# State-space phase with scans and step-times-B of 1024 columns, and ScalarE's silu and softplus behind all decays of a unit

## The reference

```python
uc = depthwise_conv4(x @ Win_u.T) + convb;  u = silu(uc);  z = x @ Win_z.T
dtr, Bm, Cm = split(u @ Wx.T, [8, 16, 16])
dt = softplus(dtr @ Wdt.T + bdt);  A = -exp(Alog)          # A is 256 x 16
h  = exp(dt_t * A) * h + (dt_t * u_t) * B_t                # 512 steps, for each channel and state
y_t = sum_n h[:, n] * C_t[n]
y  = (y + u * D) * silu(z);  out = y @ Wout.T
```

## Time and profile before

| | us |
|---|---|
| median of three runs | 2219.79 |
| the profiled execution | 2225.48 |
| its span, first to last instruction | 2223.7 |
| start, up to VectorE's first dt | 42.3 |
| unit (0,0), first part | 42.3 to 97.5 |
| the loop's rhythm (14 units) | 97.5 to 970.9 |
| rest of the last unit | 970.9 to 1031.6 |
| end of the last batch | 1031.6 to 1056 |
| attention and experts | 1056 to 2223.7 |

### The profile page before, as it was taken

The page is one execution under the profiler, slowest core; times in us unless marked ns, Lnnn a source line. Parts: engine busy times, 40 slices in busy tenths (PEclk is TensorE's granted clock), DMA queues, the critical chain, the costliest instruction groups (busy, mean ns, idle before and its releaser), DMA issues.

```text
span 2223.7 us, 29267 instructions
## 1 busy us (share of the span) xinstructions
PE 1614.2 (73%) x7664; PEld 938.7 (42%) x7664; DVE 1626.8 (73%) x2538; ACT 1174.6 (53%) x1906; POOL 1233.7 (55%) x1097
## 2 busy tenths in 40 slices
PE   3677676766677666765376887877879888897888
PEld 1445454544455444544133343443434434343443
DVE  3999999999999999996262738456384654837455
ACT  4565555656565555561146391754727357282751
POOL 2777677777777677774336280643717346181541
PEclk8888777877888777775567598898989989899999
DMA  4212022121212011120301000000100001000000
GB/s 149 82 77 84 21 82 81 76 95 76 95 76 91 21 74 81 76 91 12 115 6 36 11 27 11 16 35 16 36 8 9 34 16 36 16 10 26 11 0 15
DMA packets 39620, 107.23 MB, mean 48 GB/s; under 512 B 4128, under 2 KB 30048, under 8 KB 34368
## 3 DMA queue, kind: packets, MB, share of 16 engines
q1 hardware_dynamic: 39520, 106.24, 12.6%
HBM read 92.99 MB, written 8.65 MB: 46 GB/s over the span
## 4 chain that ended last, share of the span: by engine, by line
issue 25%; POOL 13%; PE 6%; DVE 4%; DMA 2%; ACT 1%; SPq 0%; POOLq 0%; DVEq 0%; ACTq 0%
POOL pp L1892 9%; DMA k<-k_scratch 1%; DVE mx L1583 1%; PE pbk L1224 1%; PE po L1231 1%; PE pa L1218 1%; PE og L1167 1%; PE scores L1119 1%; PE scores L1117 1%; POOL ln_r L1822 0%; DVE rec L1611 0%; POOL kp L1855 0%; ACT pt L1414 0%; POOL rotk L1851 0%; PE scores L1147 0%
## 5 line engine op out<-in xcount | busy, mean ns | idle before, releaser
L731 POOL TENSOR_TENSOR hc<-hb,cb 128x512 f32<-128x512 f32 x512 | 653.8, 1295 | 249.3 <-DVE hb L610 221.4
L610 DVE TENSOR_TENSOR_SCAN hb<-da,dbu 128x512 f32<-128x512 f32 x512 | 599.5, 1202 | 5.6 <-DVE stats L635 4.0
L499 ACT ACTIVATE da<-dt,a_neg 128x512 f32<-128x512 f32 x512 | 351.9, 717 | 352.9 <-DVE hb L610 303.9
L331 PE MATMUL yp<-ident,hc 128*128 128x128 f32 x2048 | 359.0, 317 | 65.0 <-POOL hc L731 64.6
L1892 POOL TENSOR_TENSOR pp<-pt,pp 128x512 f16<-128x512 f32 x320 | 365.0, 1151 | 71.7 <-ACT pt L1414 71.3
L331 PEld LDWEIGHTS yp<-ident,hc 128*128 128x128 f32 x2048 | 297.9, 166 | 174.3 <-POOL hc L731 93.2
L603 DVE TENSOR_TENSOR dbu<-dtu,bp 128x512 f32<-128x512 f32 x512 | 323.8, 677 | 4.0 <-PE bp L319 3.2
L1583 DVE TENSOR_REDUCE mx<-scores 128x1 f32<-128x384 f32 (+3 forms) x352 | 218.4, 636 | 131.0 <-PE scores L1119 127.9
L1693 DVE SCALAR_TENSOR_TENSOR ga<-th,pa 128x512 f32<-128x512 f32 x128 | 87.6, 685 | 246.4 <-ACT th L1429 246.4
L1413 ACT ACTIVATE pp<-scores,lift 128x512 f16<-128x512 f32 x320 | 221.5, 692 | 46.3 <-PE scores L1147 45.4
L319 PE MATMUL bp<-st,sel 96*128 96x512 bf16 x256 | 116.4, 455 | 151.7 <-DVE dbu L603 149.0
(11 more groups left out here) (181 smaller groups left out, 2265.6 us busy)
## 6 DMA issues: line engine op xcount, KB each, us to landing
cb<-c_scratch SPq DMA_DIRECT2D x16, 3072.0 KB, 11.8
cb<-c_scratch SPq DMA_DIRECT2D x16, 1024.0 KB, 4.6
q<-q_scratch SPq DMA_DIRECT2D x24, 288.0 KB
q_scratch<-qp SPq DMA_DIRECT2D x24, 128.0 KB
q<-q_scratch SPq DMA_DIRECT2D x24, 96.0 KB
xin<-in_x SPq DMA_DIRECT2D x8, 256.0 KB, 11.5
xres<-xin SPq DMA_DIRECT2D x8, 256.0 KB, 2.4
xres<-xln SPq DMA_DIRECT2D x8, 256.0 KB, 2.6
```

Of the source, the lines that this page charges most:

```text
L331: last = nc.tensor.matmul(yp[:, c, h * P:(h + 1) * P], src[:, c * P:(c + 1) * P], ident[:, :], is_transpose=True, start=(s < 0 and h == 0 ...
L499: nc.scalar.activation(da[:, s % NDA, :], dt[:, d, h, :], ACT.Exp, scale=a_neg[:, d, h, n:n + 1]).then_inc(da_done, 1)
L610: nc.vector.tensor_tensor_scan(hb[:, s % NHB, :], da[:, s % NDA, :], dbu[:, s % 2, :], 0.0, ALU.mult, ALU.add).then_inc(scan_done, 1)
L731: nc.gpsimd.tensor_tensor(hc[:, s % NHC, :], hb[:, s % NHB, :], cb[:, d, s // 2, :], ALU.mult).then_inc(hc_done, 1)
```

## The change

The two halves of a state become one operation on VectorE. TensorE now writes B twice, into both halves of PSUM `dbu` (`pe_fill`); VectorE multiplies that by `dtu` in place (one `dbu` of 1024 columns) and runs one scan over 1024 columns; the decay's first column of each half is zero, so the second half starts afresh. `bp` is gone. Since `dbu` is multiplied in place, the order on VectorE is dbu, scan, dbu, scan. Eight states of decays (16 half-buffers) are in store instead of four. The buffers `hb` and `hc` hold four states each; GpSimd still does two products of 512 columns a state, after one scan. `ud` and `act_ud` are gone: TensorE multiplies u by a diagonal matrix of D, which ScalarE makes once at the start. ScalarE does all decays of a unit first and then silu, `xd` and softplus in one piece (`act_front` at 31). `cb` is held once, in four groups of 1 MB, loaded as GpSimd lets go of each. SyncE's order changes: x of batch b+2 is loaded after batch b is stored. The front's places on TensorE move.

```diff
-            nc.tensor.matmul(bp[:, n % 2, :], sel[:, n, :], st[:, d, :], start=True, stop=True).then_inc(b_ready, 1)
+        def pe_fill(pe, b, d, n):
+            pe.wait_ge(scan_done, count(scan_done, b, NS * d + n - 1))
...
+            for h in range(NH2):
+                last = nc.tensor.matmul(dbu[:, n % 2, h, :], sel[:, n, :], st[:, d, :], start=True, stop=True)
+            last.then_inc(b_ready, 1)
...
+        def pe_front(pe, b, d, s):
+            if s == 13 and d == 0:
+                pe_xt(pe, b)
+            for i in range(NH2 * NTAP):
+                if s == (14, 15, 15, 16, 17, 18, 18, 19)[i] + 2 * (d == 0):
+                    pe_u(pe, b, d, i)
+            if s == 22:
+                pe_z(pe, b, d, 0)
+                pe_z(pe, b, d, 1)
+            if s == 23:
+                pe_xd(pe, b, d)
+            if s in (25, 26):
+                pe_dt(pe, b, d, s - 25)
...
-        def act_ud(act, b, d, h):
...
         def act_da(act, b, d, s):
-            act.wait_ge(scan_done, count(scan_done, b, STEPS * d + s + 1 - NDA))
-            nc.scalar.activation(da[:, s % NDA, :], dt[:, d, h, :], ACT.Exp,
+            if h == 0:
+                act.wait_ge(scan_done, count(scan_done, b, NS * d + n + 1 - NDA))
+            nc.scalar.activation(da[:, n % NDA, h, 1:], dt[:, d, h, 1:], ACT.Exp,
...
-            if at == 25:
+            if at == 31:
                 act_silu_u(act, b, d, 0)
...
+                act_xd(act, b, d, 0)
+                act_xd(act, b, d, 1)
+                act_xd(act, b, d, 2)
+                act_xd(act, b, d, 3)
                 for h in range(NH2):
                     for k in range(4):
                         act_soft(act, b, d, h, k)
...
+        def dve_dbu(dve, b, d, n):
...
+            nc.vector.tensor_tensor(dbu[:, n % 2], dtu[:, d], dbu[:, n % 2], ALU.mult).then_inc(dbu_done, 1)
+        def dve_scan(dve, b, d, n):
+            dve.wait_ge(dbu_done, count(dbu_done, b, NS * d + n + 1))
+            dve.wait_ge(da_done, count(da_done, b, STEPS * d + 2 * n + 2))
+            dve.wait_ge(hc_done, count(hc_done, b, NS * d + n + 1 - NHB))
...
         def dve_unit(dve, b, d, front=None, tail=None):
-            dve_dbu(dve, b, d, 0)
-            dve_dbu(dve, b, d, 1)
-            for s in range(STEPS):
+            for n in range(NS):
+                dve_dbu(dve, b, d, n)
...
+                dve_scan(dve, b, d, n)
+                if tail and n == LAG_N:
                     dve_yg(dve, *tail)
+                if tail and tail[1] == 1 and n in (9, 10, 11, 13):
+                    dve_end(dve, tail[0], {9: 0, 10: 1, 11: 2, 13: 3}[n])
...
+                if front and n == NS - 2:
+                    dve_dt(dve, *front, 0)
+                    dve_dt(dve, *front, 1)
...
         def pool_hc(pool, b, d, n):
+            for h in range(NH2):
+                last = nc.gpsimd.tensor_tensor(hc[:, n % NHC, h], hb[:, n % NHB, h * SEQ:(h + 1) * SEQ],
+                                               cb[:, n, :], ALU.mult)
+            last.then_inc(hc_done, 1)
```

More of the change, by code:

```diff
@@ L157, in mamba_phase @@
         consts_set = sems.enter_context(nc.semaphore("consts_set"))
+        da_zeroed = sems.enter_context(nc.semaphore("da_zeroed"))
+        diag_set = sems.enter_context(nc.semaphore("diag_set"))
         x_loaded = sig("x_loaded", 16)
@@ L161, in mamba_phase @@
         c_written = sig("c_written", 32, "sync")
-        c_first = sig("c_first", 32, "sync")
-        c_rest = sig("c_rest", 32, "sync")
+        c_group = [sig(f"c_group{g}", 32, "sync") for g in range(NGROUP)]
         x1_stored = sig("x1_stored", 16, "sync")
@@ L241, in sp_store, with sp_batch @@
                          x1t[:, :, :].rearrange("p (a c) m -> p a c m", a=1)).then_inc(x1_stored, 16)
+        def sp_batch(sp, b, last=False):
+            sp_c_write(sp, b + 1, 0)
+            for g in range(NGROUP):
+                sp_c_load(sp, b + 1, 0, g)
+            sp_c_write(sp, b + 1, 1)
+            for g in range(NGROUP - 1):
+                sp_c_load(sp, b + 1, 1, g)
+            sp_store(sp, b)
+            sp_keep(sp, b + 1)
+            if not last:
+                sp_x_load(sp, b + 2)
+            sp_c_load(sp, b + 1, 1, NGROUP - 1)
         @block.sync
@@ L249, in _ @@
                 sp.dma_start(dst[...], w[name]).then_inc(weights_loaded, 16)
-            sp_c(sp, 0, 0)
+            sp_c_write(sp, 0, 0)
+            for g in range(NGROUP):
+                sp_c_load(sp, 0, 0, g)
             sp_keep(sp, 0)
-            sp_c(sp, 0, 1)
-            with sp.Fori(0, NB - 1) as b:
-                sp_x_load(sp, b + 1)
-                sp_c(sp, b + 1, 0)
-                sp_store(sp, b)
-                sp_keep(sp, b + 1)
-                sp_c(sp, b + 1, 1)
+            sp_x_load(sp, 1)
+            sp_c_write(sp, 0, 1)
+            for g in range(NGROUP):
+                sp_c_load(sp, 0, 1, g)
+            with sp.Fori(0, NB - 2) as b:
+                sp_batch(sp, b)
+            sp_batch(sp, NB - 2, last=True)
             sp_store(sp, NB - 1)
@@ L375, in pe_unit @@
-                if s >= LAG_Y + 2:
-                    pe_y(pe, b, d, s - LAG_Y)
-                if tail and s == 7:
+                n = s // 2
+                if s % 2 == 0:
+                    if n + 1 < NS:
+                        pe_fill(pe, b, d, n + 1)
+                    elif after:
+                        pe_fill(pe, *after, 0)
+                else:
+                    if n < LAG_N and tail:
+                        pe_y(pe, *tail, NS - LAG_N + n)
+                    if n == LAG_N + 1:
+                        for m in range(-1, n - LAG_N):
+                            pe_y(pe, b, d, m)
+                    if n > LAG_N:
+                        pe_y(pe, b, d, n - LAG_N)
@@ L393, in pe_unit @@
             if not after:
-                for s in range(STEPS - LAG_Y, STEPS):
-                    pe_y(pe, b, d, s)
+                for n in range(NS - LAG_N, NS):
+                    pe_y(pe, b, d, n)
         @block.tensor
@@ L526, in act_front @@
                         act_soft(act, b, d, h, k)
-                for h in range(NH2):
-                    act_ud(act, b, d, h)
         def act_unit(act, b, d, front=None, tail=None):
@@ L547, in _ @@
             nc.scalar.activation(sel[:, :, :], sel32, ACT.Copy).then_inc(sel_cast, 1)
-            for at in range(16, STEPS):
+            for d in range(NDIR):
+                for h in range(NH2):
+                    nc.scalar.activation(diag_d[:, d, h, :], ident[:, :], ACT.Copy,
+                                         scale=col[:, d, h, 2:3]).then_inc(diag_set, 1)
+            for at in range(STEPS):
                 act_front(act, 0, 0, at)
```

204 lines of the change are left out of this document (78 added, 126 removed).

## The result

The changed kernel takes 2322.76 us (median of 4 runs, 2317.07 to 2326.0) against 2219.65 (4 runs on the same chip), a ratio of 1.045 [1.042, 1.049]: 103 us slower. Its profiled execution took 2317.07 us, with a span of 2314.9, 91 more than before's 2223.7.

The account below looks back on a forecast made before the run. VectorE, busy 99% of the state-space loop, was taken as the bound. 44.8 + 0.6 + 2.1 - 5.5 + 19.6 + 3 + 2 = +66.6 us on 2219.8 gave 2286 us (chance 0.52), range 2232 to 2340.

Parts of the forecast that it names:

- A state in the loop 3.62: VectorE's dbu 1.21, gap 0.22 and scan 2.19 us, 0.20 more than before; +44.8 us over 224 states.
- the gap of 0.22: VectorE idle between dbu and scan in the loop: 0.04 us signal plus two queue instructions at 0.09 each.
- Outside 3.44: A state on VectorE in units (0,0) and (7,1), where waits are constants: 0.02 us more each, +0.6 us over 32.
- The product in place: VectorE's dbu multiplied from PSUM to the same PSUM: no difference taken; an extra 0.05 us a state would be 13 us.
- The free wait: Rival: VectorE's queue hides signal and registers, a state costs 3.31 us, the whole 2199 us; chance 0.10.
- The wait for `res`, 7 x 2.8 = 19.6: VectorE's next dbu waits in 7 units for a fill behind TensorE's convolution product that needs `res`; +19.6 us, lower end +11.
- Stats bubbles gone, -5.5: VectorE's idle times between stats and scan go, since a dbu now lies between: 4.0 + 1.5, -5.5 us.
- end, +2: At the state-space phase's end the last scan is whole before GpSimd starts, so yg starts some 1.9 us later: +2.
- The front late: Rival: TensorE's lower clock delays silu and softplus, VectorE stalls 3.4 us before dt in 14 units; 2330 us, chance 0.18.
- the +3 of the sum: VectorE's dt waiting for ScalarE's softplus where TensorE runs partly at its lower clock: +3 us over 14 units.
- dt and dtu, +2.1: On VectorE they now stand back to back: dt's whole 1.53 for 1.47 us plus a wait, 15 x 0.15 = +2.1 us.
- The attention phase counted as unchanged: The phase after the state-space phase has the same code, so no difference was put in the sum.

Follow-up runs that it names:

- e4: Changed kernel with dbu and scan each cut again into two of 512 columns, order dbu, dbu, scan, scan; 2291.54 us, 1.031 of the kernel before.
- b1: Kernel before, halves of 512 columns, with dbu and scan in turn where it had dbu, dbu, scan, scan; 2303.49 us, 1.035 of the kernel before.
- e1: Changed kernel with the scan's waits for decays and GpSimd moved in front of the dbu; 2304.67 us, 1.037 of the kernel before.
- e2: Changed kernel with GpSimd held before its products 3, 4, 13 and 14 until VectorE's xln, xn, x1t and dtu are done; 2263.0 us, ratio 1.017 to before.
- e5: Changed kernel with scan's waits ahead of dbu, GpSimd held until xln, xn, x1t, dtu are done, and later u products; 2234.61 us, 1.005 of before.
- e6: Changed kernel with GpSimd held, later u products, and dbu and scan in halves of 512 instead of waits ahead; 2224.7 us, 1.000 of before.
- e8: Changed kernel, 1024 columns, VectorE order dbu, dbu, scan, scan over two states, GpSimd held before product 14, later u products, paired fills; 2269.81 us, 1.021 of before.

## Why the prediction was right or wrong, point by point

- *A state in the loop 3.62.* 3.60, so 224 x 0.182 = 40.8 us for 44.8. Right, the gap of 0.22 being 0.19: 0.03 for the signal where 0.04 was forecast, and 0.16 for two instructions where 0.18 was. *Outside 3.44*: right. *The product in place*: nothing (e4). The mechanism was tested with three doses: two, one and no instruction behind the wait that is met last give 0.19, 0.13 and 0.03. The reason given, some 0.09 for each such instruction, holds in all of them, b1 included, to within 0.03.
- *The free wait* (the Trainium skill, "VectorE: DVE Perf Modes", sections on the DRAIN and the rules for kernel authors: the semaphore costs nothing, shown there with eight copies in a row, and fewer operations win). The trace disagrees for a scan right behind its product: 41.0 us of idle time in 207 places, and b1, with the same operations as before and only the order changed, starts attention 80 us later. A consumer directly behind its producer costs 0.03 + 0.09 = 0.12 to 0.19 + 0.09 = 0.28 us here. A start saved was put at 0.05; the scan gives 421.52 - 419.32 = 2.20 us for 1024 columns against 2.24 for two of 512, which is 0.04.
- *The wait for `res`, 7 x 2.8 = 19.6*: 19.1, in seven waits of 2.17 to 3.02. Right, TensorE's lower clock included (granted 0.54). With the four waits that follow, dbu waits 22.6 us for TensorE where it waited 3.2 before: 19.4 more.
- *Stats bubbles gone, -5.5; end, +2*: both as said. yg waited 4.63 us, where it had waited 2.66.
- *The front late*, the likeliest rival: it did not come. dt waited for ScalarE in one of the 14 units of the loop, its first: 0.98 us, and then took 3.32 us instead of 1.20, since GpSimd had begun. That is about the +3 of the sum. It was close: e1, e2, e4, e5, e6 and e8 wait there in five to seven units of the loop, once the phase is quicker.
- *dt and dtu, +2.1*: this term is mis-sized (dtu alone has 13.3 us more), and a larger one the sum does not have at all. "A group has the length that it had" was assumed, without being said, for all of xln, xn, x1t, dt and dtu; they took **58 us more**, since the change moved GpSimd's product over them. In the kernel before xln and xn stood behind two dbu, where GpSimd had nearly finished; now they stand right behind the scan whose end starts 2.5 us of GpSimd. e2 takes this back. The Trainium skill ("SBUF — State Buffer", section "Who interferes with whom") has the rule: a VectorE instruction with two SBUF inputs, or in a 2-port mode, and GpSimd cannot hold the shared port pair together, and the one that comes second waits. The runs agree in that dbu, with one input in PSUM, stays at its length beside GpSimd (1211 ns), and xln, x1t, dtu and a dt that comes second do not. Nor do all instructions with SBUF on both sides grow: the four stats of `res` have one input, in SBUF, and keep 0.85 us for four beside GpSimd's products (501.62 us, GpSimd from 501.87), as they have without; the runs show no ports, only who slows whom.
- *The attention phase counted as unchanged*: wrong by -27.7 us in the profiled executions; the medians would have it at 103 - 119 = -16, an estimate that takes the state-space phase as equally long in every run.

The sum then reads: 40.8 + 0.9 (32 states outside the loop, 3.44 for 3.41) + 19.4 + 58 + 1.0 (dt) - 5.5 + 2 = 116.6 of the 118.9 us (2.3 unassigned), less 27.7. That the forecast of 2286 lay within 37 us is in part luck: the state-space phase was 52 us longer than forecast, and what the attention phase lost stands against it. The measured time also lies near the 2330 of the late front, and the range reached that far on account of it, but the time came from GpSimd's hold on VectorE, which no rival had.

## What to carry to other kernels

Halving the number of operations on the engine that bounds a kernel gains only their starts (here 0.04 us for a scan); what the new order puts side by side can cost more (0.28 us a state, and 58 us beside GpSimd), so write down for each instruction which one it reads from and what the *other* engine does at that moment. An instruction of a kind that grows beside GpSimd (here products of two SBUF tensors, and the normalising TENSOR_SCALAR from SBUF to SBUF, but not the statistics) belongs where GpSimd is idle, and a deliberate wait on GpSimd can be the cheapest repair. Where an instruction must stand right behind its producer, see in the instruction list that the wait for it sits on the instruction itself. When a repair gains less than it should, read the list of waits again: the remainder was here a wait of the same engine one step later, or a record that had grown.
